# Moving quad 1's outer streams ahead of half of quad 0's middle rows, turning the last kernel stream in two halves, and making stream 1's weights in two parts

## The reference

```
x = x + conv9x9(groupnorm(x), gaussian_kernels(weight)) + bias      # zero padding of 4
x = x + conv5x5(groupnorm(x), weight1)                              # reflected padding, through an FFT
gaussian: q = ia*xx^2 + 2*ib*xx*yy + id*yy^2 ; ker = exp(-q/2) ; ker / sum(ker)
groupnorm: 16 groups of 2 channels, (v - mean) / sqrt(var + 1e-5)
```

## Time and profile before

| | before |
|---|---|
| median of 3 runs | 240.60 us |
| profiled execution | 241.09 us, span of its instructions 239.3 us |
| TensorE (PE) busy | 232.4 us, 97% |
| VectorE (DVE) busy | 211.6 us, 88% |
| ScalarE (ACT) busy | 157.8 us, 66% |
| granted TensorE clock | 1.00 (of 2.4 GHz) |

### The profile page before, as it was taken

The page is one execution under the profiler, slowest core; times in us unless marked ns, Lnnn a source line. Parts: engine busy times, 40 slices in busy tenths (PEclk is TensorE's granted clock), DMA queues, the critical chain, the costliest instruction groups (busy, mean ns, idle before and its releaser), DMA issues.

```text
span 239.3 us, 4173 instructions
## 1 busy us (share of the span) xinstructions
PE 232.4 (97%) x1451; PEld 144.9 (61%) x1451; DVE 211.6 (88%) x460; ACT 157.8 (66%) x329; POOL 4.5 (2%) x12
## 2 busy tenths in 40 slices
PE   7999999999799999999999999999999999999995
PEld 7755656556466665556666665556666665555554
DVE  5989999898999999999989999999997459978943
ACT  6879899889489577999637694537459003569310
POOL 1000000230000000000000000000000000000000
PEclk9999999999999999999999999999999999999999
DMA  6980122320034000003422000162020002521123
GB/s 207 370 354 5 25 64 55 75 48 3 0 92 123 3 1 0 3 0 101 131 85 94 5 4 0 29 175 112 1 101 0 0 0 57 157 102 57 47 99 99
DMA packets 8709, 17.24 MB, mean 72 GB/s; under 512 B 3312, under 2 KB 5616, under 8 KB 8688
## 3 DMA queue, kind: packets, MB, share of 16 engines
q1 hardware_dynamic: 7712, 16.64, 21.1%
q10 hardware_dynamic: 976, 0.34, 0.6%
HBM read 5.57 MB, written 4.72 MB: 43 GB/s over the span
## 4 chain that ended last, share of the span: by engine, by line
PE 57%; DVE 26%; ACT 8%; issue 5%; DMA 3%; SPq 0%; DVEq 0%; ACTq 0%
PE banks L1508 29%; PE banks L1491 28%; DVE X L805 5%; DVE lo L772 3%; DMA X<-in_x 3%; ACT junk L1108 3%; DVE whl L565 2%; DVE wl L590 1%; ACT P L1141 1%; ACT hi L1164 1%; DVE work L560 1%; ACT arg L1188 1%; DVE arg L548 1%; ACT work L1206 1%; DVE X L812 1%
## 5 line engine op out<-in xcount | busy, mean ns | idle before, releaser
L1491 PE MATMUL banks<-hi,whl 128*128 128x360 f16 (+4 forms) x576 | 98.0, 318 | 2.2 <-ACT hi L1164 1.5
L1491 PEld LDWEIGHTS banks<-hi,whl 128*128 128x128 f16 x576 | 55.5, 98 | 36.7 <-issue 1.9
L1491 PE MATMUL banks<-lo,whl 128*128 128x376 f16 (+4 forms) x288 | 51.2, 318 | 0.0
L1108 ACT ACTIVATE junk<-X 128x576 bf16<-128x576 f32 x56 | 41.2, 737 | 2.8 <-DMA X<-in_x 0.8
L1491 PEld LDWEIGHTS banks<-lo,whl 128*128 128x128 f16 x288 | 27.9, 97 | 16.6
L1508 PE MATMUL banks<-hi,wh 128*128 128x384 f16 (+1 forms) x165 | 31.5, 320 | 0.2 <-ACT hi L1164 0.2
L1508 PE MATMUL banks<-lo,wh 128*128 128x384 f16 (+1 forms) x165 | 31.5, 320 | 0.0
L1508 PE MATMUL banks<-hi,wl 128*128 128x384 f16 (+1 forms) x165 | 31.5, 320 | 0.0
L1164 ACT CAST hi<-work 128x416 f16<-128x416 f32 x32 | 16.6, 536 | 16.9 <-PE banks L1508 11.9
L1154 ACT ACTIVATE work<-work,gof,gsc 128x26 f32<-128x26 f32 (+1 forms) x48 | 24.9, 609 | 3.6 <-DVE gof L666 3.6
L1164 ACT CAST hi<-s 128x384 f16<-128x384 f32 x32 | 15.4, 508 | 17.2 <-DVE s L739 10.9
(11 more groups left out here) (137 smaller groups left out, 233.4 us busy)
## 6 DMA issues: line engine op xcount, KB each, us to landing
X<-in_x SPq DMA_DIRECT2D x8, 576.0 KB, 10.1
out<-X SPq DMA_DIRECT2D x7, 576.0 KB, 2.8
work<-X SPq DMA_DIRECT2D x8, 432.0 KB, 3.8
whl<-work SPq DMA_DIRECT2D x24, 64.0 KB, 2.0
work<-X SPq DMA_DIRECT2D x8, 144.0 KB, 3.6
stage<-in_w SPq DMA_DIRECT2D x1, 640.0 KB, 8.0
work<-X SPq DMA_DIRECT2D x32, 12.0 KB, 2.3
out<-X SPq DMA_DIRECT2D x1, 384.0 KB, 2.6
```

Source lines behind the costliest of these rows:

```text
L1108: nc.scalar.activation(waste, image(n, m), function, accum_out=sums[c][:, col:col + 1]).then_inc(sums_done[c], 1)
L1491: ins = nc.tensor.matmul(dst[:, :, y0:y1], w[1][:, i, t * P:(t + 1) * P], src[:, :, y0 + IMG * dx:y1 + IMG * dx], start=(first and part == ...
```

## The change

Three things are changed. Stream 1's float32 scaling and its cast are made in two parts, taps 2 to 4 and then taps 0 and 1, as stream 2's were; `casts` counts the additional cast, and `conv1` waits for a second value of `wh1_done` ahead of tap 1 for both streams. The DMAs of stream 6's turned taps are issued in two groups of four, for the high and the low half, with a semaphore of their own for the low half. On VectorE, `streams1_ends(1)` goes ahead of `rows1(0, 1)`, and the low halves of these streams between the even and the odd rows.

```diff
+SPLIT = (1, 2)
+LAST_TURNED = MIRROR[FIRST_ORDER[-1]]
 def casts(i):
     at = FIRST_ORDER.index(i)
-    return at + 1 + (1 if at >= FIRST_ORDER.index(2) else 0)
+    return at + 1 + sum(at >= FIRST_ORDER.index(j) for j in SPLIT)
...
+            def turn_half(at, i, half, landed):
+                sp.wait_ge(turning, 2 * (at - len(TURN_BANKS)) + half + 1)
+                for k in range(RB):
+                    sp.dma_start(whl[(RB - 1 - k) * C:(RB - k) * C, half, MIRROR[i], NT * P:],
+                                 turn_at[k * C:(k + 1) * C, at % TURNS, half, :]).then_inc(landed, 16)
-            for at, i in enumerate(FIRST_ORDER):
+            for at, i in enumerate(FIRST_ORDER[:-1]):
                 if i not in TURN_BANKS:
                     turn(at, i)
+            turn_half(7, FIRST_ORDER[-1], 0, turned[LAST_TURNED])
+            turn_half(7, FIRST_ORDER[-1], 1, last_low_turned)
...
-                flat1 = slot(1).rearrange("p k (r o) -> p (k r) o", o=C)
-                done(stt(flat1, flat1, W_SCALE, krec[...].to_broadcast([P, NT * RB, C]), ALU.mult, ALU.mult))
-                MARK["weights", 1] = count[0]
+                for half, taps in enumerate(STEPS2):
+                    at = slice(*taps)
+                    flat1 = slot(1)[:, at, :].rearrange("p k (r o) -> p (k r) o", o=C)
+                    done(stt(flat1, flat1, W_SCALE, krec[...].to_broadcast([P, (taps[1] - taps[0]) * RB, C]), ALU.mult, ALU.mult))
+                    MARK["weights", 1, half] = count[0]
...
                 far1(1)
-                rows1(0, 1)
                 streams1_ends(1)
+                rows1(0, 1, (0,))
                 low_halves(1, 1, range(2, 4))
+                rows1(0, 1, (1,))
                 middle1(0, 2)
...
-            high_kernel(1)
+            high_kernel_parts(1)
...
-            high_kernel_two()
+            high_kernel_parts(2)
...
                     elif qd == 0 and first and part == 0:
-                        pe.wait_ge(wh1_done, casts(i) - (1 if i == 2 else 0))
+                        pe.wait_ge(wh1_done, casts(i) - (1 if i in SPLIT else 0))
...
+                    if qd == 0 and not first and part == 2 and i == LAST_TURNED:
+                        pe.wait_ge(last_low_turned, 16 * RB)
                     for t in taps:
-                        if qd == 0 and first and part == 0 and i == 2 and t == STEPS2[1][1] - 1:
+                        if qd == 0 and first and part == 0 and i in SPLIT and t == STEPS2[1][1] - 1:
                             pe.wait_ge(wh1_done, casts(2))
```

More of the change, by code:

```diff
@@ L264, in build @@
         turned = {i: sem(f"turned{i}") for i in range(8)}
+        last_low_turned = sem("last_low_turned")
         hi_done = {c: sem(f"hi{c}_done") for c in (1, 2)}
@@ L796, in middle1, with rows1 @@
                 stt(pd[1][:, :], product1(qd, k), -f, mb[1][:, :], ALU.mult, ALU.add).then_inc(mid_done[1], 1)
-            def rows1(qd, g):
-                for which, src, factors in ((0, ps, EVEN_ROWS), (1, pd, ODD_ROWS)):
+            def rows1(qd, g, halves=(0, 1)):
+                for which in halves:
+                    src, factors = ((ps, EVEN_ROWS), (pd, ODD_ROWS))[which]
                     dve.wait_ge(mid_done[1], 6 * qd + 2 * g + which + 1)
@@ L890, in first_quad @@
                 dve.wait_ge(dve_w, MARK["krec"])
-                flat1 = slot(1).rearrange("p k (r o) -> p (k r) o", o=C)
-                done(stt(flat1, flat1, W_SCALE, krec[:, :].unsqueeze(1).to_broadcast([P, NT * RB, C]), ALU.mult, ALU.mult))
-                MARK["weights", 1] = count[0]
+                for half, taps in enumerate(STEPS2):
+                    at = slice(*taps)
+                    flat1 = slot(1)[:, at, :].rearrange("p k (r o) -> p (k r) o", o=C)
+                    done(stt(flat1, flat1, W_SCALE, krec[:, :].unsqueeze(1).to_broadcast([P, (taps[1] - taps[0]) * RB, C]), ALU.mult, ALU.mult))
+                    MARK["weights", 1, half] = count[0]
                 kernel_scale()
@@ L1192, in high_kernel, with high_kernel_parts @@
                 nc.scalar.copy(made_taps(wh, i), weight1(i)).then_inc(wh1_done, 1)
-            def high_kernel_two():
+            def high_kernel_parts(i):
                 for step, taps in enumerate(STEPS2):
                     at = slice(*taps)
-                    act.wait_ge(dve_w, MARK["weights", 2, step])
-                    nc.scalar.copy(made_taps(wh, 2)[:, at, :], slot(2)[:, at, :]).then_inc(wh1_done, 1)
+                    act.wait_ge(dve_w, MARK["weights", i, step])
+                    nc.scalar.copy(made_taps(wh, i)[:, at, :], slot(i)[:, at, :]).then_inc(wh1_done, 1)
             def turn_kernel(i, part):
```

## The result

The changed kernel took 242.75 us in the median of four executions (242.62 to 243.34) against 240.76 us of the kernel before. The ratio of the times is 1.0086, with a 95% interval of [1.0067, 1.0105]. That is 2.0 us slower; 242.5 was forecast. The profiled execution has a span of 241.0 us, of 242.76 us in all.

A forecast was written before the change was run, and what follows sets the result against it. The VectorE/ScalarE chain was taken to bound the kernel up to 99.9 us, TensorE alone from 100.05 us. +2.1 (tap 1 wait) - 0.2 (VectorE's pause) + 0 (turned halves) = +1.9 us: 240.6 to 242.5 us, 80% range 241.4 to 244.0.

The forecast's parts named there:

- The wait at tap 1: TensorE in stream 1, near 18.7 us, stalls 2.54 us for stream 2's last cast; 2.1 us reach the VectorE/ScalarE chain.
- The room of 0.41 us: ScalarE's 0.17 us before the copy at 23.93 us and 0.24 before stream 0's cast cover a stall up to 0.41 us.
- The way into the chain: ScalarE's copy of stream 2's turned weights, ahead of stream 0's cast at 24.64 us, passes on 2.13 us to VectorE.
- The first rival: TensorE's own slack, not the VectorE/ScalarE chain, takes the stall; end moves -0.2 to +0.2 us, 240.6 us; chance 7 in 100.
- The outer streams first: TensorE's 1.31 us wait near 64 us moves to stream 5; only VectorE's lost pause counts, 0.2 us gained (bounds 0 and 0.4).
- the -0.2 us of VectorE's pause: VectorE loses its pause before the low halves at 63.79 us, 0.1 to 0.2 us; 0.2 taken as gain.
- The turned halves: Last turned stream near 52 us: TensorE gains 0.1 to 0.3 us, hidden by its next waits, so 0 at the end.
- The sum: Whole kernel: +2.1 (wait at tap 1) - 0.2 (VectorE's pause) + 0 (turned halves) = +1.9 us, giving 242.5 us.
- VectorE's 0.07 us: Scaling stream 1's weights in two parts, before 17.04 us, costs VectorE some 0.07 us more.
- The clock rival: TensorE's clock falls to 1.2 GHz behind the tap 1 stall: 1.5 to 4.5 us more, 2 as middle, 244.5 us; chance 9 in 100.

The follow-up runs named there:

- the first experiment: The changed kernel with the wait ahead of tap 1 asking for the stream's own casts instead of stream 2's; 240.66 us, ratio 1.0008.
- the second experiment: The kernel before with one edit: TensorE, ahead of tap 1 of stream 1's first part, also waits for all of stream 2's casts; 243.15 us, ratio 1.0115.
- the experiment with the cast ahead of the copy: The changed kernel with its long wait, ScalarE casting stream 0's data before copying stream 2's turned high weights; 242.07 us, ratio 1.0076.
- the wait alone: Same run as the second experiment: the kernel before with only the added wait for stream 2's casts ahead of tap 1; 243.15 us, ratio 1.0115.

## Why the prediction was right, point by point

**The wait at tap 1: right, in cause and size.** Forecast were a stall of 2.54 us, ScalarE idle for 1.2 and 0.7 to 1.2 us and stream 0's cast 2.1 us late; the traces show 2.50 us of lateness behind the reciprocal, 1.21 and 1.07 us, and 2.12 us. The idle time printed beside the stall, 1.95 us, is shorter because TensorE itself was 0.37 us later against VectorE in this execution and the ends of matmuls overlap. Two small things were off. The sum has 21.21 us where its terms, 21.18 and 0.05, give 21.23; and ScalarE's casts of stream 2 were 0.18 us earlier behind the reciprocal than before (4.45 against 4.63), not 0.1. The first and the second experiment show from both sides that this edit is all of the slowdown.

**The room of 0.41 us: right**, 0.38 in four kernels.

**The way into the chain: right but not whole.** ScalarE's program order carried the 2.1 us, yet it is not the only way: with it out of the way the matmul of the statistics carried 1.0 us of the same lateness. The first rival (the late TensorE is swallowed) was therefore priced too low. It let the lateness be swallowed in TensorE's own waits; by the experiment with the cast ahead of the copy, about 1.0 us would have come in at the statistics.

**The outer streams first: mis-sized by its only term.** TensorE's 1.31 us came back before stream 5 as forecast. But the -0.2 us of VectorE's pause was not won. The old pause before the low halves went; a new one of 0.2 us stands at 66.40 us, where the middle products wait for the rows that now stand right before them (63.84 to 66.40 us is 2.56 us for work of 2.35). The failing step is this: I had counted the pause that the move closes and not the one it opens. The experiment with the low halves behind all rows wins those 0.2 us.

**The turned halves: worth nothing, as forecast**, with less moved than I gave it: TensorE stands 0.38 us before the low weights (at 55.05 us) instead of 0.40 before the high ones, where 0.1 to 0.3 was forecast. The eight DMAs take 590 ns each to issue:

```profile
L425 SPq DMA_DIRECT2D whl<-work x8: 590/590/592, 48.7 to 53.1; - x8
...
DMA to landing us min/median/max: 1.8/1.9/1.9
```

The last starts at 53.1 us, 3.0 us behind the old last one, of which 1.7 are the common shift, so it is 1.3 us later and not 1.0. A transfer of half the size lands in 1.9 instead of 2.0 us, so halving the data did not pay for the four issues more.

**The sum.** +2.12 + 0.00 = 2.1 us against +1.9 forecast, of which the profiled execution shows 1.7, since its weights began 0.46 us earlier; the ratio gives 2.1 us (240.6 x 0.0086). The -0.2 that failed is small beside the rest: without it the forecast would have been 2.1. VectorE's 0.07 us for the second part of the scaling stands in the forecast's text but not in its sum. The long wait hides it here; the first experiment shows it, with stream 0's cast 8.87 us behind the reciprocal instead of 8.80 and released by VectorE's stream.

**The clock rival: a real mechanism.** It was given 9 in 100. In the changed kernel's four executions none is 1.6 us over the others, and all have a clock of 1.00, so it had no part in the 2.0 us; with so few executions that is in part luck. One of four of the wait alone (244.44 us) and one of four with ScalarE's cast first (243.66 us) are 1.6 us over the others, both with a mean granted clock of 0.993. Over the kernels with this long stall that makes 9 of 35 executions. Its price was put at 1.5 to 4.5 us, with 2 as a middle; it was 1.6.

## What to carry to other kernels

When a wait's threshold is made to apply to a second user, work out the count for each user: here a wait that names another stream's work ran without a hang, and cost what lies between the two, less the room. Before pricing a stall on the busiest engine, look for what sits behind it in program order on the others, and for every such place, since closing one uncovers the next. A saving on TensorE ahead of a point where another chain releases it was worth nothing here, and a move on that chain was worth the pauses that it closed less those that it opened.

## What the runs showed of the hardware that was not expected

A stall of TensorE of 1.9 to 2.5 us can take its clock to 1.2 GHz or not, in the same kernel: 7 of 23 executions of one kernel were 1.6 us over the others, all seven with a mean granted clock of 0.992 or 0.993 and the sixteen others at 0.999 or 1.000, and a profiled one shows the granted clock at 0.79 over 8 us. A wait of 4.70 us took it there in all eight executions (0.985 to 0.993). GpSimd's sum of two float32 tensors of 128x640 took 3.1 and 3.6 us beside VectorE's work, against 1.35 us on VectorE (2.70 us for two), and stretched VectorE's two-input instructions beside it from 0.96 to 3.4 us. A VectorE instruction that waits for the one right before it had a pause of 0.2 us ahead of it (at 66.40 us in the changed kernel).
